# A decoder layer's state-space scan: the opening before the first quad, rebuilt

## Time and profile before

| what | value |
|---|---|
| median of three runs | 2993.81 us |
| the profiled execution | 2995.75 us |
| its span | 2993.6 us |
| PE busy | 2732.6 us (91%) |
| DVE busy | 2552.1 us (85%) |
| POOL busy | 1925.1 us (64%) |
| ACT busy | 1692.0 us (57%) |

### The profile page before, as it was taken

How to read it: one execution, slowest core, us unless ns; L and a number is a source line. 1 busy time by engine, 2 the same in 40 slices (tenths; PEclk the granted TensorE clock), 3 DMA queues, 4 the chain that set the end, 5 groups by cost and what they waited for, 6 DMA issues and landing times.

```text
span 2993.6 us, 35283 instructions
## 1 busy us (share of the span) xinstructions
PE 2732.6 (91%) x11120; PEld 1562.5 (52%) x11120; DVE 2552.1 (85%) x3521; ACT 1692.0 (57%) x2848; POOL 1925.1 (64%) x884
## 2 busy tenths in 40 slices
PE   8968899999989999998999888788889999999996
PEld 4535555555555555555555455455544555555553
DVE  2259899999999999999999999999966787787785
ACT  2356566575656657565565755656534555555553
POOL 1159897888979788896988988889841222222221
PEclk9989899999999999999999999898999999999998
DMA  5432333434343343424333322432401211111110
GB/s 176 134 101 81 97 88 104 147 89 129 92 134 114 99 143 90 132 85 157 94 108 104 99 87 73 133 86 65 118 29 37 97 56 56 63 56 56 63 63 22
DMA packets 132876, 281.32 MB, mean 94 GB/s; under 512 B 12528, under 2 KB 12656, under 8 KB 132224
## 3 DMA queue, kind: packets, MB, share of 16 engines
q1 hardware_dynamic: 132736, 279.59, 30.4%
HBM read 245.86 MB, written 33.69 MB: 93 GB/s over the span
## 4 chain that ended last, share of the span: by engine, by line
PE 54%; DVE 31%; issue 9%; ACT 4%; POOL 1%; DMA 0%; DVEq 0%; ACTq 0%; POOLq 0%; SPq 0%
DVE arena L1262 17%; PE banks L473 15%; PE banks L497 9%; DVE arena L1278 7%; PE banks L567 7%; PE banks L707 4%; PE banks L660 4%; PE banks L616 3%; PE banks L641 3%; PE banks L510 2%; PE banks L671 2%; PE banks L631 2%; ACT banks L1023 2%; DVE arena L1218 1%; PE banks L714 1%
## 5 line engine op out<-in xcount | busy, mean ns | idle before, releaser
L1186 POOL TENSOR_TENSOR arena<-arena 128x2048 f32<-128x2048 f32 x256 | 1161.8, 4539 | 79.8 <-PE banks L567 79.7
L1262 DVE TENSOR_TENSOR_SCAN arena<-banks,arena 128x512 f32<-128x512 f32 x1024 | 1185.4, 1205 | 19.2 <-POOL arena L1186 16.2
L1023 ACT ACTIVATE banks<-arena,a_sb 128x508 f32<-128x508 f32 x1024 | 696.9, 684 | 734.5 <-DVE arena L1262 734.1
L473 PE MATMUL banks<-arena 128*128 128x512 f32 x2048 | 952.9, 603 | 11.0 <-DMA arena<-in_xT 8.1
L567 PEld LDWEIGHTS banks<-ident,arena 128*128 128x128 f32 x4096 | 493.6, 146 | 418.6 <-issue 197.7
L567 PE MATMUL banks<-ident,arena 128*128 128x128 f32 x4096 | 576.2, 284 | 139.4 <-DVE arena L1278 72.6
L473 PEld LDWEIGHTS banks<-arena 128*128 128x128 f32 x2048 | 373.1, 195 | 363.8 <-issue 360.5
L1278 DVE SCALAR_TENSOR_TENSOR arena<-banks,cg,arena 128x512 f32<-128x512 f32 x640 | 453.0, 739 | 72.4 <-PE banks L567 71.6
L497 PE MATMUL banks<-arena 128*128 128x512 f32 x1024 | 472.3, 600 | 5.2 <-DMA arena<-in_WoutT 3.9
L1132 POOL TENSOR_TENSOR arena<-arena 128x512 f32<-128x512 f32 x240 | 306.0, 1275 | 205.3 <-ACT arena L851 204.1
L1199 POOL TENSOR_TENSOR arena<-arena 128x512 f32<-128x512 f32 x128 | 141.2, 1103 | 434.6 <-DVE arena L1434 434.5
(11 more groups left out here) (137 smaller groups left out, 2977.1 us busy)
## 6 DMA issues: line engine op xcount, KB each, us to landing
arena<-b_scratch SPq DMA_DIRECT2D x128, 512.0 KB, 5.1
arena<-in_WinX SPq DMA_DIRECT2D x128, 256.0 KB, 2.9
arena<-in_WinZ SPq DMA_DIRECT2D x128, 256.0 KB, 2.7
...
arena<-x_scratch SPq DMA_DIRECT2D x32, 512.0 KB, 3.4
...
```

What stands on the lines that cost most here:

```text
L473: last = nc.tensor.matmul(home(kind, i), wr[w % 2][:, k, :], x[:, k, :], start=(k == 0), stop=(k == KC - 1))
L1023: nc.scalar.activation(by_seq(bank(i % 2))[:, :, 1:SEQ], by_seq(dt[s % 2][:, i, :])[:, :, 1:SEQ], ACT.Exp, scale=a_sb[:, QD * q + i, n:n + ...
L1186: nc.gpsimd.tensor_tensor(hb[n % 4].rearrange("p (i t) -> p i t", i=QD), dtu, brep[pair % 3][:, n % 2:n % 2 + 1, :].broadcast_to([P, QD, G ...
L1262: nc.vector.tensor_tensor_scan(h, bank(i % 2), h, 0.0, ALU.mult, ALU.add)\
```

## The change

The opening now runs X tiles 0 to 15 before B's rows, tile 16 beside them, and tile 17 after the first D; tiles 17 to 19 and tile 16's last steps are finished inside quad 0. `pe_ssm` moves into the tile two after its pair. Quad 0 gets an order of its own (`OPENING`, 84 pieces): 4 pieces ahead of the first turn, and the other 80 in the stretches of indices 0 to 12, none in the last three. ACT takes an X tile's four instructions one after the other. dt * u of quad 0 is made by DVE, tile by tile (`dve_dtu`); the products of index 0 by POOL, tile by tile (`pool_opening`); those of index 1 by DVE, after the scans of index 0. The copy of C moves ahead of the first dt, tile 17's taps behind the scans of index 1. SP and ACT get orders of their own for quad 0 (`sync_opening`, `act_opening`). Quads 1 to 15 and the rest are as before.

```diff
@@ -56,6 +56,9 @@
 LEAD = 5 * QD
+EARLY = DT + 2
+HEAD = 4
+OPENING = "X-2 X-1 Z0 X0 D0 Z1 X1 D1 D2 Z2 D3 X2 Z3 X3".split()
 ORDER = ["Z0 X0 Z1 D0 X1 D1 Z2 D2 O0 O1 O2 O3 D3 X2 Z3 X3 O4 O5 O6 O7".split()] * (NQ - 1) + \
-SPACE = 100
+OPEN = sum([(5, 4), (3, 3), (3, 3), (3, 3), (3, 3), (3, 3), (3, 3), (3, 3), (3, 3), (3, 3), (2, 3), (3, 3), (3, 3)], ())
+def order(s):
+    return ORDER[s % NQ] if s else OPENING
 def jobs():
-    found = [("X", m) for m in range(LEAD)] + [("D", i) for i in range(QD)]
+    found = [("X", m) for m in range(EARLY - 1)] + [("D", i) for i in range(QD)] + [("X", EARLY - 1)]
     for s in range(NS):
-        found += [j for j in (job(s, name) for name in ORDER[s % NQ]) if j]
+        found += [j for j in (job(s, name) for name in order(s)) if j]
         found += [("Y", QD * s + i) for i in range(QD)]
     return found + [("O", 2 * QD * (NS - 1) + c) for c in range(2 * QD)]
@@ -304,6 +311,8 @@
                 return
             g = s // NQ
             after(sp, "bm_ok", N * s + 2 * j + 2 - 6)
+            if s == 0 and j == 3:
+                sp.wait_ge(S["bm_two"], QD)
             sp.wait_ge(S["b_stored"], 16 * (g + 1))
             r = (N // 2 * s + j) % 3
@@ -426,6 +435,50 @@
             if mine:
                 sync_store_u(sp, X[2])
 
+        def sync_opening(sp):
+
+            X = LEAD
+            sync_ahead(sp, "X", X - 3, 0)
+            sync_ahead(sp, "X", X - 3, 1)
+            sync_u(sp, 1)
+            sync_wdt(sp, 1)
+            sync_ahead(sp, "X", X - 2, 0)
+            sync_store_u(sp, X - 4)
+            sync_b(sp, 0, 3)
+            sync_ahead(sp, "X", X - 2, 1)
+            sync_store_u(sp, X - 3)
+            sync_ahead(sp, "X", X - 1, 0)
+            sync_b(sp, 0, 4)
...
         def pe_filler(pe, s, p):
-            sizes = SIZES[s % NQ]
+            sizes = SIZES[s % NQ] if s else (HEAD,) + OPEN
             lo, hi = sum(sizes[:p]), sum(sizes[:p + 1])
             start = 0
-            for name in ORDER[s % NQ]:
+            for name in order(s):
                 found = job(s, name)
                 for k in range(STEPS[name[0]]):
@@ -570,18 +623,24 @@
                     last.then_inc(S["t_done"], 1)
 
                 pe.wait_ge(S["scan_ok"], QD * (U + 1))
-                if n == 2 and (has_x(s - 1) or s == 0):
+                if s == 0 and n in (3, 6):
+                    pe.wait_ge(S["ss_added"], DT // 2 + 1 + n // 6)
+                if n == 2 and has_x(s - 1):
                     pe.wait_ge(S["ss_added"], (LEAD + QD * s) // 2)
                 if n == 5 and q == NQ - 1 and s + 1 < NS:
                     pe.wait_ge(S["bt_rows"], g + 2)
                 if n == 12 and has_x(s):
                     pe.wait_ge(S["ss_added"], (LEAD + QD * s) // 2 + 1)
+                past = 1 if s == 0 else 0
                 turn(0)
                 turn(1)
-                pe_filler(pe, s, 2 * n)
+                pe_filler(pe, s, 2 * n + past)
                 turn(2)
                 turn(3)
-                if n == 1 and (has_x(s - 1) or s == 0):
+                if s == 0 and n in (2, 5):
+                    pe.wait_ge(S["acc_ok"], kept(s, n, SPLIT))
+                    pe_ssm(pe, DT // 2 + n // 5)
+                if n == 1 and has_x(s - 1):
                     pe.wait_ge(S["acc_ok"], kept(s, n, SPLIT))
@@ -795,7 +854,9 @@
         def act_dt_abs(act, j):
             s = j // QD
             act.wait_ge(S["dt_mm"], j + 1)
-            after(act, "dtu_ok", s - 1)
+            if s == 2:
+                act.wait_ge(S["dtu_part"], QD)
+            after(act, "dtu_ok", s - 2)
             nc.scalar.activation(dt[s % 2][:, j % QD, :], home("D", j), ACT.Abs).then_inc(S["dt_abs"], 1)
 
+        def act_opening(act, n, slot):
+
+            X, D = LEAD, QD
+            e = 4 * n + slot
+            if e == 3:
+                act_x_exp(act, X - 4)
+                act_x_ln(act, X - 4)
+                act_x_sig(act, X - 4)
+            if e == 4:
+                act_base(act, X - 3)
+            if e == 8:
+                act_base(act, X - 2)
+                act_x_exp(act, X - 3)
+            if e == 9:
+                act_x_ln(act, X - 3)
...
+                act_base(act, X)
+            if e == 29:
+                act_dt_abs(act, D)
+                act_dt_exp(act, D)
+            if e == 30:
+                act_dt_ln(act, D)
+            if e == 32:
+                act_x_exp(act, X)
+            if e == 33:
+                act_z_copy(act, 1)
+                act_x_ln(act, X)
+            if e == 34:
+                act_z_exp(act, 1)
+                act_z_ln(act, 1)
+            if e == 35:
+                act_z_sig(act, 1)
...
+            if e == 49:
+                act_dt_exp(act, D + 3)
+                act_dt_ln(act, D + 3)
+            if e == 50:
+                act_z_sig(act, 2)
+
@@ -1148,17 +1293,30 @@
             pool.wait_ge(S["z_sig"], j + 1)
             nc.gpsimd.tensor_tensor(v, v, sgz, ALU.mult).then_inc(S["z_ok"], 1)
 
+        def pool_opening(pool):
+
+            pool.wait_ge(S["brep_loaded0"], 16)
+            for i in range(QD):
+                pool.wait_ge(S["dtu_part"], i + 1)
+                nc.gpsimd.tensor_tensor(hb[0][:, i * GT:(i + 1) * GT], dtu[:, i, :], brep[0][:, 0, :], ALU.mult)\
+                    .then_inc(S["bm_part" if i < QD - 1 else "bm_ok"], 1)
+
         def pool_step(pool, s):
             g, q = divmod(s, NQ)
             mine, mined = has_x(s), has_x(s - 1)
             Z, X = QD * s, LEAD + QD * s
-            pool.wait_ge(S["dt_ok"], QD * (s + 1))
-            pool.wait_ge(S[f"u_loaded{s % 2}"], 16 * (s // 2 + 1))
-            after(pool, "bm_ok", N * s)
-            nc.gpsimd.tensor_tensor(dtu, dt[s % 2], uq[s % 2], ALU.mult).then_inc(S["dtu_ok"], 1)
-            pool.wait_ge(S["dtu_ok"], s + 1)
+            if s > 0:
+                pool.wait_ge(S["dt_ok"], QD * (s + 1))
+                pool.wait_ge(S[f"u_loaded{s % 2}"], 16 * (s // 2 + 1))
+                pool.wait_ge(S["bm_ok"], N * s)
+                nc.gpsimd.tensor_tensor(dtu, dt[s % 2], uq[s % 2], ALU.mult).then_inc(S["dtu_ok"], 1)
+                pool.wait_ge(S["dtu_ok"], s)
             for n in range(N):
                 U = N * s + n
+                if U == 0:
+                    pool_opening(pool)
+                if U < 2:
+                    continue
                 if U >= 4:
                     pool_sums(pool, (U - 4) // N, (U - 4) % N)
                     if (U - 4) % N in SHARED:
@@ -1167,15 +1325,17 @@
                     pool_z(pool, Z - 1)
                 if n == 1 and mined:
                     pool_u(pool, X - 2)
-                if n == 3 and (mined or s == 0):
+                if n == 3 and mined:
                     pool_u(pool, X - 1)
-                if n == 6:
+                if s == 0 and n in (3, 4, 5, 7):
+                    pool_u(pool, X - 4 + (3, 4, 5, 7).index(n))
+                if n == (8 if s == 0 else 6):
                     pool_z(pool, Z)
-                if n == (8 if q < NQ - 1 else 11):
+                if n == (8 if q < NQ - 1 and s > 0 else 11):
                     pool_z(pool, Z + 1)
                 if n == 10 and mine:
                     pool_u(pool, X)
-                if n == (12 if q < NQ - 1 else 14):
+                if n == (12 if q < NQ - 1 and s > 0 else 14):
                 if q == 1 and g > 0 and n == 5:
                     pool_rstd(pool, g - 1)
 
@@ -1253,9 +1413,20 @@
             nc.vector.scalar_tensor_tensor(d, home("D", j), 0.0, d, ALU.max, ALU.add)\
                 .then_inc(S["dt_ok"], 1)
 
+        def dve_dtu(dve, i):
+
+            dve.wait_ge(S["dt_ok"], i + 1)
+            dve.wait_ge(S["u_loaded0"], 16)
+            nc.vector.tensor_tensor(dtu[:, i, :], dt[0][:, i, :], uq[0][:, i, :], ALU.mult)\
+                .then_inc(S["dtu_part"], 1)
+
         def dve_scan(dve, U, i):
 
-            if i == 0:
+            if U == 1:
+                dve.wait_ge(S["bm_two"], i + 1)
+            elif U == 0 and i < QD - 1:
+                dve.wait_ge(S["bm_part"], i + 1)
+            elif i == 0 or U == 0:
                 dve.wait_ge(S["bm_ok"], U + 1)
             dve.wait_ge(S["exp_ok"], QD * U + i + 1)
             h = hb[U % 4][:, i * GT:(i + 1) * GT]
@@ -1325,17 +1496,21 @@
+            if n == 1 and mined:
                 dve_ss_add(dve, X // 2 - 1)
+            if s == 0 and n in (2, 5):
+                dve_ss_add(dve, DT // 2 + n // 5)
+            if s == 0 and n in (0, 3, 5, 7):
+                dve_taps(dve, X - 2 + (0, 3, 5, 7).index(n))
             if n == 2 and late and more:
                 dve_ss_stats(dve, g + 1)
             if n == 2 and q == 1 and g > 0:
                 dve_ln_shift(dve, g - 1)
             if n == 4 and late and more:
                 dve_rows(dve, g + 1)
-            if n == 3 and mine:
+            if n == 3 and mine and s > 0:
                 dve_taps(dve, X)
-            if n == (8 if late else 5) and mine:
```

(81 more changed lines are left out.)

93 lines of the change are left out of this document (84 added, 9 removed).

## The result

| | before | changed |
|---|---|---|
| median (14 runs each) | 2993.93 us (2992.56 to 2997.57) | 2988.06 us (2987.01 to 2991.67) |
| ratio | | 0.9981, 95% interval 0.9974 to 0.9988 |
| profiled execution / span | 2995.75 / 2993.6 us | 2988.28 / 2986.3 us |

The change gains 5.9 us; the forecast was 13.1 us. The sign was right, the size less than half.

A forecast was written before the change was run, and what follows sets the result against it. DVE's entry into quad 0 was taken to count: 18.0 us earlier, less 4.9 of added DVE work, is 13.1 off the profiled 2995.75, so 2982.7; the median 1.9 lower, 2980.7. Range 2969.5 to 2988.5.

The forecast's parts named there:

- Tile 16 starts at the same time as before: 16 tiles and seven ssm precede it both times: Opening, on PE: tile 16 starts at 132.7 us, as before the change.
- 141.1, 5.2, 0.6 and 0.7: Opening: last ssm ends at 141.1; 5.2 us from sum to last scaling, 0.6 for transposes, about 0.7 for tsb's copy.
- It fits, with 5 us to spare, as in quad 1: Quad 0, indices 0 to 12: PE needs 93 us and 3 for a half-clock start; DVE has 101 us.
- added work: Inside quad 0, DVE gets two more tiles' taps (2.2 each) and one more sum (0.5): 4.9 us.
- rival 2: Quad 0: PE sets the pace, late turns make DVE wait; five us more, perhaps eight, 2986 to 2989; chance 0.14.
- the hold of DVE's four products: Before quad 0: index 1's products on DVE alternate with POOL's instructions, ending at 177.1, not 168.0; chance 0.46.
- Rival 1: Before quad 0: no hold, or DVE's four products in one run after index 2's; 2971.5 or 2974.9; chance 0.27.
- the way from tsb to the entry: End of the opening: tsb copied at 148.1, DVE enters quad 0 at 184.0, where before it was 202.0.
- the clock and quads 1 to 15: PE's granted clock not under 0.9 in indices 0 to 12; after quad 0 nothing changes, the shift lasts to the end.
- slower outcome: Quad 0: PE stays at 1.2 GHz for part of the first thirteen indices; 3007 with a third; chance 0.05.
- Q: Interval from DVE's entry into quad 0 to the first Y transpose; 118.55 us before, 123.45 with the forecast's 4.9.
- E: Interval from the start of tsb's copy to DVE's entry into quad 0; the forecast had 35.9 from the copy's end.

The follow-up runs named there:

- e3: Against the changed kernel, the ssm of tiles 2 and 3 stands three pieces later; 2985.73 us, ratio 0.9971 to the kernel before.
- e1: Against the changed kernel, POOL's products of index 2 wait until DVE's four products of index 1 are done; 2979.10 us.
- e2: Against the changed kernel, index 1's products go back to POOL, all four tiles in one instruction; 2978.31 us.
- e8: Against the changed kernel, two of eight pieces of each X and Z tile of quad 0 are left out; 2988.77 us.
- e9: Against the changed kernel, only quad 0's order altered: PE pieces moved between stretches, ACT's z_sig of Z1 and x_sig of tile 20 one slot later; 2982.71 us.
- e4: Against the changed kernel, one PE piece moved from index 8's second stretch to index 10's first; 2985.81 us.
- e6: Against the changed kernel, ACT copies B's row 1 into a PSUM bank, from which DVE makes index 1's products; 2977.02 us.
- e10: Against the changed kernel, the edits of e1, e3 and e9 together; 2971.80 us.
- e11: Against the changed kernel, the edits of e6, e3 and e9 together; 2971.99 us.

## Why the prediction was wrong, and where it was right

**Wrong: "Tile 16 starts at the same time as before: 16 tiles and seven ssm precede it both times".** Tile 16 started at 136.9, 4.2 us late. The amount of work was right, but the change moves every ssm earlier, and for the second of them, at 49.38 us, its u isn't there: ACT's base of tile 3 waits until 42.89 for the store of tile 0's u to DRAM, as it did before (42.74), when the ssm stood at 53.17 and nothing hung on it. The forecast had put this wait at nothing. The stop and, in some executions, the lower clock behind it made tsb start at 152.17; moving that one ssm (e3) gives 148.14. This is 4.0 us of the miss, 1.1 to 3.1 in executions in which the clock holds (tsb at 149.27 to 151.21 in e1, e2, e8, e9). Another 0.7 us are left in e3 too, where tsb is done at 148.83 and not at 148.1: the last ssm ends 0.3 later than forecast, and the four transposes take 1.06 us instead of 0.6, after 4.55 us in which PE stood idle. (The forecast's own terms, 141.1, 5.2, 0.6 and 0.7, make 147.6; it put 0.5 us on top of them without a source.)

**Wrong: "It fits, with 5 us to spare, as in quad 1".** PE's sum of 93 us was not the mistake; with 12 us less it is no faster (e8). An average over thirteen indices cannot show a stretch of 5 us between two pairs of turns, a turn behind ACT's part, a bank that is freed late. These cost 5.0 of the 5.6 us, added work that was put 0.6 too low the rest; they are the mechanism half named in rival 2 ("a late turn makes DVE wait, which has to be paid even where the sums are equal"), with its size, 5 us more, and without its premise, that PE is full. e9, which has e4's piece in it, gave 4.95 back. This is the larger of the two steps that failed.

**Right: the hold of DVE's four products.** Forecast from 1 us holds: one product after each of POOL's three instructions, 11.7 us from the end of index 0's scans. Measured 11.03, with the order of the instructions as forecast. Rival 1 is refuted in the change; its four short products are what e1 and e6 have (2.47 and 2.46 us).

**Right: the way from tsb to the entry.** Forecast 148.1 to 184.0, 35.9 us from the end of the copy; measured 152.86 to 188.31, 35.45 us. Inside it, errors cancel, which is luck: the last scan of index 0 ended 17.9 us after tsb, not 17.3, since the first one waited 2.85 us for ACT, which does all dt tiles before the first exponential (the loads of B, issued 1.58 instead of 3.04 us after the store, would have let it start 1.2 us sooner: POOL's first product was done at 162.0, the scan started at 163.19); the hold was 0.7 shorter than forecast, and the scans and taps behind it took 6.6 us instead of 6.9.

**Right: the clock and quads 1 to 15.** 0.90 in the stretch of quad 0, as before; no slower outcome. But the forecast carried the shift through to the end unchanged, and 4 us came back on the way: 1.4 between quad 0 and quad 1, where half of the transposes of Y ran at full clock (0.49 us instead of 0.84), 1.5 between the Y transposes of quads 2 and 3, nothing from there to those of quad 15, and 1.2 behind them. In all twelve kernels with the new opening the lead in the span is larger than at the first Y transpose, by 2.5 (e11) to 6.8 us (e8). The reason stays open, and no term of the forecast stands for it.

**The sum.** -4.8 (tsb done), +0.5 (from there to the entry), -5.6 (Q) makes -9.9 against the forecast, and 13.1 - 9.9 = 3.2 us is the lead at the first Y transpose; about 4 were returned behind it: 7.3 in the span, 5.9 in the medians. With these three orders mended, but the hold left in, the kernel would take e10's 2971.8 + 8.6 = 2980.4 us, worked out from E and not run; the forecast was 2980.7. That this comes so close is luck in part: in e10 with a hold of 8.6 us the lead at the first Y transpose would be 10.6 us, 2.5 under the forecast's 13.1, and 6.0 us more came in e10 behind it.
